# A two-layer graph kernel: scalar-tensor-tensor forms on VectorE, diagonal cells set among the incoming scatters, one branch on TensorE and GpSimd

## The chip, the core and the metric

The kernel runs on one core of one Trainium2 chip. The metric is the device time of one execution in microseconds, as the median of several runs. A core has TensorE (PE in the rows: matmul, with its weight loads as PEld), VectorE (DVE), ScalarE (ACT), GpSimd (POOL) and SyncE (SP), each with its own instruction stream, and 16 DMA engines. The streams meet only at semaphores. SBUF is the core's working memory, PSUM holds what TensorE accumulates, in 8 banks of 512 floats on each partition.

## What is computed

x has 1250 nodes of 1024 features, and there are 20,000 edges (src, dst), sorted by dst. Two layers follow each other, each with a residual and a layernorm.

```
def _sage_layer(h, edge_src, edge_dst, deg_inv, W_self, W_neigh, b):
    agg = jax.ops.segment_sum(h[edge_src], edge_dst, num_segments=h.shape[0])
    mean = agg * deg_inv[:, None]
    return h @ W_self + mean @ W_neigh + b
h = relu(_sage_layer(x, src, dst, deg_inv, W_self0, W_neigh0, b0))
x = _layernorm(x + _sage_layer(h, src, dst, deg_inv, W_self1, W_neigh1, b1))
# GCN layer over the same edges and one loop for each node
h = x @ W.T + b;  norm = deg_inv_sqrt[row] * deg_inv_sqrt[col]
x = _layernorm(x + segment_sum(norm[:, None] * h[col], row))
```

deg_inv is 1/max(number of incoming edges, 1), and deg_inv_sqrt comes from the out-degree plus one.

## The kernel before

The sums over edges are made dense. Two tables in HBM, `adj_in` and `adj_out`, hold for each pair of nodes how many edges there are; TensorE multiplies by them. A table has 1280 x 1280 cells, in five panels of 256 target nodes. All work is in float32 kept as a high and a low part (`hi`, `lo`: the rounded value, and what is left of it), so that one product takes three or two matmuls.

**GpSimd** builds the tables. It clears `adj_in` by four DMAs (`clear`), reads a flag that VectorE has computed (`general`: the edges are not of the usual kind; with these inputs it is 0), and then issues 160 indirect DMAs into `adj_in`, 125 cells each (`put`, line 643): ten groups g of 16. A group needs the indices that VectorE makes for it (`repeats(g)`, semaphore `batch_ready`). In the middle of group 0 it issues the four DMAs that clear `adj_out`. After group 9 it waits for `cleared_out`, sets the diagonal of `adj_out` to one by two DMAs of 640 single cells each (line 673), waits for both (`diagonal_set`), and issues 160 more scatters, into `adj_out`. "Incoming" and "outgoing" scatters are those into `adj_in` and `adj_out`. The scatters of groups 0 to 2, 3 to 6, 7 and 8, and 9 count on four semaphores, `scattered_in[0]` to `[3]` (`NEEDS`).

**TensorE** runs these stages in order: transposes of x with x @ W_neigh0 (`linear(N0, t)`, lines 1417 and 1446); x @ W_self0 turned (`self_turned`, 1472); the first mean by `adj_in` (`mean0`, lines 1492 and 1503) in four chunks of 2, 4, 2 and 2 tiles of 128 nodes, each with ten matmuls for the degrees and then eight blocks d of 128 features; the second layer's two weight products by seven products in place of eight, Strassen-like (`products(0)` and `products(1)`, 1560); the second mean (`mean1`, 1577); the GCN sum by `adj_out` (`gather`, 1594, in the same four chunks); and the GCN weights (`linear(GCN, t)`, 1417 and 1401). Mean0, mean1 and gather exist twice in the program, for the usual form and for the general one, which takes plain float32; TensorE branches on the flag at line 1641 ahead of mean0 and at line 1647 ahead of mean1 and gather. In both the general form stands first in the program, so the usual one is jumped to.

**VectorE** takes what TensorE accumulated and splits it: the low part is `tensor_tensor(value, hi, subtract)`. In mean0 it multiplies each block by 1/degree, which frees the PSUM bank (`h_free`), and adds the self part, which SP fetched (`s0_in`); TensorE may be six blocks ahead of it: `pe.wait_ge(h_free, m - 5)` for block m counted from 0, so its ninth block needs the third multiply. After the second block of chunk 0 VectorE also reduces a panel (line 1185). Ahead of the products and of mean1 TensorE waits for low parts (`right_lo`, `u1_lo_done`; lines 1074 and 1160).

**SP** loads in one fixed order. `load_chunk_1(c)` waits for the scatters that chunk c needs:

```
for b in range(c + 1):
    sp.wait_ge(scattered_in[b], 16 * RUN * (NEEDS[b] - (NEEDS[b - 1] if b else 0)))
load_panels(adj_in, c, m1_panels[c], m1_full)
```

Chunk 1 therefore needs groups 0 to 6, 112 scatters, and the fetches of the self part for mean0 stand behind it in SP's stream. The first load of `adj_out` waits for all 160 outgoing scatters (`scattered_out`) and for the ninth tile of mean1. ScalarE makes the high parts.

Of the kernel before, what the change touches and what calls it, by code (L numbers as in the profile page):

```python
# [6 lines left out]
T = 128  # L7
# [8 lines left out]
F32 = mybir.dt.float32  # L16
# [7 lines left out]
def build(nc, x, src, dst, w_self0, w_neigh0, b0, w_self1, w_neigh1, b1, w_gcn, b_gcn, out):  # L24
# [44 lines left out]
    with ExitStack() as ctx:  # L69
# [542 lines left out]
        def _(pool):  # L612
# [37 lines left out]
            with pool.If(general > 0):  # L650
# [12 lines left out]
            pool.wait_ge(cleared_in, 16 * 4)  # L663
            for g in range(GROUPS):
                pool.wait_ge(batch_ready, g + 1)
                for c in range(RUN):
                    put(adj_in, idx_in, mult, g * RUN + c, scattered_in[sum(g >= need for need in NEEDS)])
                    if (g, c) == (0, RUN // 2):
                        clear(adj_out, cleared_out)
# [5 lines left out]
            for j in range(EC):  # L675
                put(adj_out, idx_out, loops, j, scattered_out)
# [217 lines left out]
        def _(dve):  # L894
# [7 lines left out]

            def grouped(buf):
                return buf[0:EP, :].rearrange("p (g c) -> p g c", g=GROUPS)
# [6 lines left out]
            def split_lo(l, k):  # L911
                dve.wait_ge(w_hi_done, KD * l + k + 1)
                nc.vector.tensor_tensor(w_row(l, k, 1), raw_slots[raw_slot[l, k]], w_row(l, k, 0).bitcast(F32), ALU.subtract
                                        ).then_inc(w_lo_done, 1)
# [52 lines left out]
            def repeats(g):  # L967
# [5 lines left out]
                for k, (first, found) in enumerate(((0, before), (WINDOW + 1, behind))):  # L973
                    near = key[0:EP, g, first:first + RUN]
                    near = bass.AP(tensor=near.tensor, offset=near.offset, ap=[*near.ap, [1, WINDOW]])
                    nc.vector.tensor_tensor(eq, mine, near, ALU.is_equal).then_inc(same, 1)
# [95 lines left out]
            def right_low(n):  # L1072
                dve.wait_ge(right_hi, n + 1)
                nc.vector.tensor_tensor(right_op[n % 2][:, :, 1, :], rights[n // 7][n % 7], right_op[n % 2][:, :, 0, :].bitcast(F32),  # L1074
                                        ALU.subtract).then_inc(right_lo, 1)

            def left_sums(i):
# [4 lines left out]
                elif i == 1:  # L1082
                    dve.wait_ge(left_sum, 1)
                    nc.vector.tensor_tensor(a21, a11, a21, ALU.subtract).then_inc(left_sum, 1)
# [4 lines left out]
                else:  # L1089
                    dve.wait_ge(left_sum, 3)  # L1090
                    dve.wait_ge(left_lo, 2)
                    nc.vector.tensor_tensor(a12, a12, a11, ALU.subtract).then_inc(left_sum, 1)
# [586 lines left out]
```

## Time and profile before

| | us |
|---|---|
| median of 3 runs (lowest, highest) | 856.4 (853.21, 860.26) |
| the profiled execution, whole | 858.52 |
| its span, first to last instruction | 856.8 |
| TensorE busy | 833.5 (97%) |
| VectorE busy | 461.7 (54%) |
| GpSimd busy | 459.5 (54%) |
| ScalarE busy | 177.4 (21%) |

The mean granted clock of TensorE is 0.993 of its full 2.4 GHz. Times in the rows are us from the span's start. An engine's "idle before" is the time in which it did nothing ahead of an instruction, and behind the arrow stands what ended last before it started; where several semaphores are waited for, only the last one is named.

### The profile page before, as it was taken

The numbers are of one execution on the slowest core, as the hardware profiler recorded it, in microseconds if no ns is written. First come the engines' busy times: TensorE is split into PE (matmuls) and PEld (weight loads), VectorE is DVE, ScalarE is ACT, GpSimd is POOL, SyncE is SP. The second block draws the span as 40 slices with busy tenths as digits, with TensorE's granted clock in tenths as the row PEclk, the third lists the DMA queues.
The fourth block names the chain that finished last, engine by engine and source line by source line (L and its number), as shares of the span: only waits on it lengthen the run. The fifth ranks groups of instructions, "written<-read, shape, count | busy, mean of one in ns | idle before, by whom it ended". The sixth has DMA issues, their size and how long they took to land.

```text
span 856.8 us, 10998 instructions
## 1 busy us (share of the span) xinstructions
PE 833.5 (97%) x4295; PEld 710.8 (83%) x4295; DVE 461.7 (54%) x714; ACT 177.4 (21%) x218; POOL 459.5 (54%) x343
## 2 busy tenths in 40 slices
PE   8999999999999999999999999999979999999996
PEld 6888888888988899788888888778869889988885
DVE  6555659200017465897553678666663535455555
ACT  4111131111111113353223012222221122200000
POOL 5028886877778857888588688878830000000000
PEclk9999999999999999999999999999999999999998
DMA  9977965453786443768886579168757748655551
GB/s 334 379 294 277 341 197 154 136 161 89 196 256 166 111 86 102 258 238 282 291 292 217 219 262 292 33 192 228 214 183 263 224 144 282 210 197 197 196 191 44
DMA packets 99482, 180.56 MB, mean 211 GB/s; under 512 B 15474, under 2 KB 75898, under 8 KB 94048
## 3 DMA queue, kind: packets, MB, share of 16 engines
q1 hardware_dynamic: 60144, 124.17, 43.6%
q10 hardware_dynamic: 26896, 40.65, 13.4%
q0 software_dynamic: 12384, 14.95, 7.7%
q8 instruction: 38, 0.62, 0.3%
q14 instruction: 20, 0.16, 0.0%
HBM read 107.08 MB, written 72.43 MB: 210 GB/s over the span
## 4 chain that ended last, share of the span: by engine, by line
POOL 46%; PE 28%; issue 20%; DMA 3%; DVE 2%; POOLq 1%; ACT 0%; SPq 0%; DVEq 0%
POOL adj_out L643 25%; POOL adj_in L643 21%; PE ps L1417 13%; PE ps L1594 10%; PE ps L1446 2%; PE ps L1401 1%; DMA adj_out<-ones_nt 1%; POOLq L643 1%; DMA panel_tiles<-adj_out 1%; DMA raw<-in_L_gnn_W_neigh 1%; DVE sacc L1291 0%; PE ps L1358 0%; DMA adj_out<-loops,idx_out 0%; DVE wx L908 0%; PE ps L1616 0%
## 5 line engine op out<-in xcount | busy, mean ns | idle before, releaser
L643 POOL DMA_INDIRECT adj_out<-loops,idx_out x160 | 245.1, 1532 | 74.1 <-issue 65.8
L643 POOL DMA_INDIRECT adj_in<-mult,idx_in x160 | 198.7, 1242 | 89.2 <-issue 89.2
L1560 PE MATMUL ps<-u 128*128 128x512 f32 x840 | 190.7, 389 | 1.4 <-DVE u L1074 1.4
L1560 PEld LDWEIGHTS ps<-u 128*128 128x128 f32 x840 | 157.6, 188 | 34.3 <-issue 1.6
L1472 PE MATMUL ps<-wx 128*128 128x512 f32 (+1 forms) x576 | 109.7, 351 | 1.2 <-ACT outb L751 1.1
L1472 PEld LDWEIGHTS ps<-wx 128*128 128x128 f32 x576 | 94.0, 189 | 17.0 <-ACT outb L751 1.8
L1417 PE MATMUL ps<-u 128*128 128x512 f32 x432 | 98.2, 389 | 0.0
L1577 PE MATMUL ps<-u,panel_tiles 128*128 128x512 f32 (+1 forms) x400 | 93.9, 393 | 1.9 <-DVE s L1141 1.9
L1503 PE MATMUL ps<-wx,u 128*128 128x256 f32 (+5 forms) x640 | 95.3, 310 | 0.0
L1417 PEld LDWEIGHTS ps<-u 128*128 128x128 f32 x432 | 81.0, 188 | 16.8
L1503 PEld LDWEIGHTS ps<-wx,u 128*128 128x128 f32 (+1 forms) x640 | 87.4, 192 | 6.6
L1417 PE MATMUL ps<-wx 128*128 128x512 f32 x384 | 89.6, 392 | 0.0
L1577 PEld LDWEIGHTS ps<-u,panel_tiles 128*128 128x128 f32 (+1 forms) x400 | 74.5, 188 | 18.0 <-issue 2.3
L1417 PEld LDWEIGHTS ps<-wx 128*128 128x128 f32 x384 | 71.4, 188 | 14.6
L1594 PE MATMUL ps<-u,wx 128*128 128x512 f32 (+2 forms) x480 | 74.5, 317 | 0.0
L1594 PEld LDWEIGHTS ps<-u,wx 128*128 128x128 f32 x480 | 67.2, 191 | 6.6
L1171 DVE TENSOR_SCALAR dinv_row<-ps 128x256 f32<-128x256 f32 (+2 forms) x4 | 1.9, 479 | 88.3 <-PE ps L1492 88.3
L834 ACT ACTIVATE std<-mv,eps 128x1 f32<-128x1 f32 x20 | 5.9, 295 | 163.5 <-DVE mv L1015 163.5
L751 ACT ACTIVATE outb<-ps,b0c 128x512 f32<-128x512 f32 (+1 forms) x24 | 14.8, 617 | 95.7 <-PE ps L1472 87.8
L1335 DVE SCALAR_TENSOR_TENSOR outb<-ps,dscale,xin 128x1024 f32<-128x1024 f32 x9 | 11.6, 1285 | 40.2 <-PE ps L1417 40.2
L806 ACT ACTIVATE ht<-ht 128x256 f32<-128x256 f32 (+2 forms) x32 | 14.9, 466 | 84.1 <-DVE ht L1182 84.1
L993 DVE TENSOR_TENSOR u<-ps,u 128x1024 fp32r<-128x1024 f32 x10 | 12.2, 1224 | 35.0 <-ACT u L711 35.0
(170 smaller groups left out, 783.8 us busy)
## 6 DMA issues: line engine op xcount, KB each, us to landing
left_scr<-u SPq DMA_DIRECT2D x7, 2560.0 KB, 9.5
u<-left_scr SPq DMA_DIRECT2D x7, 2560.0 KB, 9.6
xt_scr<-wx ACTq DMA_DIRECT2D x10, 1024.0 KB, 9.9
u<-xt_scr SPq DMA_DIRECT2D x10, 1024.0 KB, 4.9
wx<-xt_scr SPq DMA_DIRECT2D x16, 512.0 KB, 3.7
adj_in<-u POOLq DMA_DIRECT2D x4, 1600.0 KB, 24.9
adj_out<-u POOLq DMA_DIRECT2D x4, 1600.0 KB, 15.4
wx<-adj_in SPq DMA_DIRECT2D x5, 1280.0 KB, 8.0
```

The lines of the kernel that those rows point to most:

```text
L643: pool.indirect_dma_start(table, bass.IndirectOffsetOnAxis(ap=index[0:EP, j:j + 1], axis=0), counts[0:EP, j:j + 1], None, bounds_check=CEL ...
L751: nc.scalar.activation(staged[i % 4][:, 0:width], ps[:, d, 0:width], ACT.Identity, bias=b0c[:, d:d + 1]).then_inc(s0_free, 1)
L806: nc.scalar.activation(cell, cell, ACT.Relu).then_inc(h_done, 1)
L993: nc.vector.tensor_tensor(u[:, :, t, 1, :], pair_bank(acc_pair(q, t)).rearrange("p (a j) -> p a j", a=2), u[:, :, t, 0, :].bitcast(F32), A ...
L1335: nc.vector.scalar_tensor_tensor(z, pair_bank(acc_pair(GCN, t))[:, :], dscale[:, t:t + 1], rest, ALU.mult, ALU.add).then_inc(acc_free, 1)
L1417: ins = nc.tensor.matmul(acc[:, cols], left_tile[:, t % 2, k, left * T:(left + 1) * T], w_row(q, k, right)[:, cols], start=(i == 0), stop= ...
L1446: ins = nc.tensor.matmul(pair_bank(acc_pair(N0, t))[:, cols], xs[:, t, k, left * T:(left + 1) * T], w_row(N0, k, right)[:, cols], start=(k ...
L1472: ins = nc.tensor.matmul(block_of[d], w[:, k, left, d * P:(d + 1) * P], where[right], start=(first and left + right == 0), stop=(final and ...
L1503: ins = nc.tensor.matmul(ps[:, h_bank(m), 0:width].rearrange("p (n j) -> p n j", n=n // 2), typed(u0_part(k, h, d), exact), typed(panels[0 ...
L1560: ins = nc.tensor.matmul(ps[:, product_bank(g, i, p), :], left_op[n % 2][:, p, k, left, :], right_op[n % 2][:, k, right, :], start=(not on ...
L1577: ins = nc.tensor.matmul(pair_bank(acc_pair("MEAN1", t))[:, cols], typed(p1_tile[t][0:rows(k), k, :], exact), typed(u[0:rows(k), n, k, h, ...
L1594: ins = nc.tensor.matmul(ps[:, g_bank(KD * c + d), 0:width].rearrange("p (n j) -> p n j", n=n // 2), typed(yd[:, h, d * P:(d + 1) * P], ex ...
```

## The change

Three things, and no other engine's stream is touched.

First, a helper `once(out, a, b, op)` issues `scalar_tensor_tensor(out, a, 1.0, b, mult, op)`, which is a * 1.0 op b, in place of `tensor_tensor(out, a, b, op)`. It is used in 124 instructions: the low parts of weights (24), of right operands (14) and of u1 (4), the comparison of keys (20), the additions of the self part (32), of bias and self rows (10 and 10), and the operand sums (10). Low parts read from PSUM, the left operands and the sums over the products stay as they were.

Second, GpSimd sets the diagonal ahead of group 5 of the incoming scatters. The wait for `diagonal_set` stays ahead of the outgoing scatters.

Third, TensorE branches once, ahead of mean0, and all later stages stand in both arms, the usual form first. GpSimd's branch likewise has the usual form of all its scatters in the first arm.

```diff
+            def scatter(general_form):
+                def diagonal():
+                    pool.wait_ge(cleared_out, 16 * 4)
+                    for i in range(2):
+                        cells = bass.AP(tensor=adj_out.tensor, offset=i * T * (PW + 1), ap=[[PW + 1, T], [PANEL + PW * PW, NT // 2]])
+                        pool.dma_start(cells, ones_nt[:, 0:NT // 2], allow_slow_non_contiguous=True).then_inc(diagonal_set, 16)
+
+                pool.wait_ge(cleared_in, 16 * 4)
+                for g in range(GROUPS):
+                    pool.wait_ge(batch_ready, g + 1)
+                    if g == GROUPS // 2:
+                        diagonal()
+                    for c in range(RUN):
+                        put(adj_in, idx_in, mult, g * RUN + c, scattered_in[sum(g >= need for need in NEEDS)])
+                        if (g, c) == (0, RUN // 2) and not general_form:
+                            clear(adj_out, cleared_out)
+                pool.wait_ge(diagonal_set, 32)
+                for j in range(EC):
+                    put(adj_out, idx_out, loops, j, scattered_out)
+
+            with pool.If(general == 0):
+                scatter(False)
+            with pool.Else():
+                clear(adj_out, cleared_out)
...
-            pool.wait_ge(cleared_out, 16 * 4)
-            for i in range(2):
-                diagonal = bass.AP(tensor=adj_out.tensor, offset=i * T * (PW + 1), ap=[[PW + 1, T], [PANEL + PW * PW, NT // 2]])
-                pool.dma_start(diagonal, ones_nt[:, 0:NT // 2], allow_slow_non_contiguous=True).then_inc(diagonal_set, 16)
-            pool.wait_ge(diagonal_set, 32)
...
+            def once(out, a, b, op):
+                return nc.vector.scalar_tensor_tensor(out, a, 1.0, b, ALU.mult, op)
...
-                nc.vector.tensor_tensor(cell, cell, fetch_slot(m)[:, 0:width], ALU.add).then_inc(h_sum, 1)
+                once(cell, cell, fetch_slot(m)[:, 0:width], ALU.add).then_inc(h_sum, 1)
...
-            with pe.If(general > 0):
-                mean0(True)
-            with pe.Else():
-                mean0(False)
-            products(0)
-            products(1)
-            with pe.If(general > 0):
-                mean1(True)
-                gather(True)
-            with pe.Else():
-                mean1(False)
-                gather(False)
-            for t in range(NT):
-                linear(GCN, t)
+            def later_stages(exact):
+                mean0(exact)
+                products(0)
+                products(1)
+                mean1(exact)
+                gather(exact)
+                for t in range(NT):
+                    linear(GCN, t)
+
+            with pe.If(general == 0):
+                later_stages(False)
             with pe.Else():
...
+                later_stages(True)
```

GpSimd's stream from its branch on, as a difference (branch, incoming scatters, clears, diagonal, outgoing scatters; the arm that the flag 0 takes):

```order
+L670 COMPARE_AND_BRANCH
 L643 DMA adj_in<-mult,idx_in 1638400x1 x9
 L636 DMA adj_out<-u 128x3200 x4
-L643 DMA adj_in<-mult,idx_in 1638400x1 x151
-L673 DMA adj_out<-ones_nt 128x5x1 x2
+L643 DMA adj_in<-mult,idx_in 1638400x1 x71
+L655 DMA adj_out<-ones_nt 128x5x1 x2
+L643 DMA adj_in<-mult,idx_in 1638400x1 x80
 L643 DMA adj_out<-loops,idx_out 1638400x1 x160
```

The two diagonal DMAs moved from behind the 160th incoming scatter to behind the 80th, so the 32 scatters of groups 5 and 6 that chunk 1 needs stand behind them.

TensorE's stream before, from the end of mean0's second arm to the start of the second mean (1560 are the products, 1577 and 1368 mean1 and the transposes in it):

```order
L1503 MATMUL ps<-wx,u 128x226 x100
L1643 UNCONDITIONAL_BRANCH
L1560 MATMUL ps<-u 128x512 x840
L1647 COMPARE_AND_BRANCH
L1577 MATMUL ps<-u,panel_tiles 128x512 x80
L1368 MATMUL ps<-ident,late 128x128 x8
```

The same place now, in the first arm (1515 is mean0, 1572 the products, 1589 and 1380 mean1):

```order
L1515 MATMUL ps<-wx,u 128x226 x100
L1572 MATMUL ps<-u 128x512 x840
L1589 MATMUL ps<-u,panel_tiles 128x512 x80
L1380 MATMUL ps<-ident,late 128x128 x8
L1589 MATMUL ps<-u,panel_tiles 128x512 x40
```

The second compare-and-branch is gone, and what follows it in the program is the form that runs. Line numbers of VectorE and TensorE are 10 to 13 higher in the changed kernel.

## Rows read from the trace of the kernel before

**Rows 1.** The page's part 1: busy us, share of the span, instructions.
```profile
PE 833.5 (97%) x4295; PEld 710.8 (83%) x4295; DVE 461.7 (54%) x714; ACT 177.4 (21%) x218; POOL 459.5 (54%) x343
```

**Rows 2.** PE's waits: us in total, times, longest.
```profile
PE ps L1594 <- DMA panel_tiles<-adj_out: 4.5, 1, 4.5
PE ps L1492 <- ACT outb L751: 2.0, 1, 2.0
PE ps L1577 <- DVE s L1141: 1.9, 1, 1.9
```

**Rows 3.** Two lines of PE's sequencer: durations in ns, starts in us.
```profile
L1641 PEldq COMPARE_BRANCH  x1: 3933/3933/3933, 236.3 to 236.3; - x1
...
L1647 PEldq COMPARE_BRANCH  x1: 5952/5952/5952, 532.1 to 532.1; - x1
```

**Rows 4.** PE's timeline: start us, us, instruction, idle before and releaser.
```profile
345.67 1.63 PE L1560 MATMUL ps<-u 128*128 128x512 f32 x6 [1.43 <-DVE u L1074]
...
538.26 0.93 PE L1577 MATMUL ps<-u,panel_tiles 128*128 128x512 f32 x3 [1.90 <-DVE s L1141]
...
642.69 2.61 PE L1594 MATMUL ps<-panel_tiles,wx 128*128 128x256 f32 x13 [4.50 <-DMA panel_tiles<-adj_out]
```

**Rows 5.** SP's timeline, 224 to 262 us.
```profile
240.70 2.33 SPq L425 DMA_DIRECT2D wx<-adj_in  x2
```

**Rows 6.** SP's waits: us in total, times, longest.
```profile
SPq L460 <- DMA adj_in<-mult,idx_in: 22.7, 3, 12.2
```

**Rows 7.** VectorE's timeline, 242 to 266 us.
```profile
259.75 0.42 DVE L1182 TENSOR_TENSOR ht<-ht,xin 128x256 f32<-128x256 f32 x1 [5.54 <-DMA xin<-s0t_scr]
260.09 2.81 DVE L1185 TENSOR_REDUCE dpart<-wx 128x10 f32<-128x2560 f32 x1
...
263.14 0.42 DVE L1179 TENSOR_TENSOR ht<-ps,dinv_row 128x256 f32<-128x256 f32 x1
```

**Rows 8.** PE's timeline, 262 to 268 us.
```profile
265.39 2.90 PE L1503 MATMUL ps<-wx,u 128*128 128x512 f32 x12
```

**Rows 9.** GpSimd's groups by line: xcount, busy us, mean ns, idle before.
```profile
L643 POOL DMA_INDIRECT adj_out<-loops,idx_out x160 | 245.1, 1532 | 74.1 <-issue 65.8 <-DMA adj_out<-ones_nt 8.3
L643 POOL DMA_INDIRECT adj_in<-mult,idx_in x160 | 198.7, 1242 | 89.2 <-issue 89.2
...
L673 POOL DMA_DIRECT2D adj_out<-ones_nt x2 | 1.8, 926 | 0.0
```

**Rows 10.** GpSimd's timeline: two stalls, the diagonals' wait, two slow scatters.
```profile
201.48 1.19 POOL L643 DMA_INDIRECT adj_in<-mult,idx_in  x1 [2.77 <-issue]
...
322.71 1.47 POOL L643 DMA_INDIRECT adj_out<-loops,idx_out  x1 [8.34 <-DMA adj_out<-ones_nt]
...
340.99 3.29 POOL L643 DMA_INDIRECT adj_out<-loops,idx_out  x1 [0.30 <-issue]
...
415.62 1.19 POOL L643 DMA_INDIRECT adj_out<-loops,idx_out  x1 [8.95 <-issue]
...
595.24 1.70 POOL L643 DMA_INDIRECT adj_out<-loops,idx_out  x1 [0.30 <-issue]
```

**Rows 11.** VectorE's timeline ahead of the products and of the second mean.
```profile
343.13 2.28 DVE L1074 TENSOR_TENSOR u<-raw,u 128x2048 fp32r<-128x2048 f32 x1
...
533.81 2.82 DVE L1160 TENSOR_TENSOR u<-u,u 128x2560 fp32r<-128x2560 f32 x1
```

**Rows 12.** VectorE's groups by line: xcount, busy us, mean ns, idle before.
```profile
L1147 DVE TENSOR_TENSOR spare<-spare,bias 128x1024 f32<-128x1024 f32 x7 | 8.5, 1218 | 2.2 <-DMA spare<-in_x 2.2
...
L938 DVE SCALAR_TENSOR_TENSOR mult<-mult,u 125x160 f32<-125x160 f32 x2 | 0.7, 325 | 0.1
...
L923 DVE TENSOR_TENSOR mult<-mult,loops 125x160 f32<-125x160 f32 x1 | 0.3, 326 | 0.0
```

**Rows 13.** VectorE's timeline during two of the slow scatters.
```profile
340.39 2.82 DVE L1069 TENSOR_TENSOR u<-ht,u 128x2560 fp32r<-128x2560 f32 x1 [4.22 <-ACT u L775]
...
594.59 1.28 DVE L1276 SCALAR_TENSOR_TENSOR wx<-outb,dscale,wx 128x1024 fp32r<-128x1024 f32 x1 [1.59 <-ACT wx L843]
```

More of the change, by code:

```diff
@@ L662, in _ @@
                 pool.wait_ge(prescattered, 16 * EC)
[L663 to L669, printed above, removed]
-            pool.wait_ge(cleared_out, 16 * 4)
-            for i in range(2):
-                diagonal = bass.AP(tensor=adj_out.tensor, offset=i * T * (PW + 1), ap=[[PW + 1, T], [PANEL + PW * PW, NT // 2]])
-                pool.dma_start(diagonal, ones_nt[:, 0:NT // 2], allow_slow_non_contiguous=True).then_inc(diagonal_set, 16)
-            pool.wait_ge(diagonal_set, 32)
-            for j in range(EC):
-                put(adj_out, idx_out, loops, j, scattered_out)
+                scatter(True)
         @block.scalar
@@ L975, in repeats @@
                     near = bass.AP(tensor=near.tensor, offset=near.offset, ap=[*near.ap, [1, WINDOW]])
-                    nc.vector.tensor_tensor(eq, mine, near, ALU.is_equal).then_inc(same, 1)
+                    once(eq, mine, near, ALU.is_equal).then_inc(same, 1)
                     dve.wait_ge(same, g * STEPS + 2 * k + 1)
@@ L1083, in left_sums @@
                     dve.wait_ge(left_sum, 1)
-                    nc.vector.tensor_tensor(a21, a11, a21, ALU.subtract).then_inc(left_sum, 1)
+                    once(a21, a11, a21, ALU.subtract).then_inc(left_sum, 1)
                 elif i == 2:
@@ L1091, in left_sums @@
                     dve.wait_ge(left_lo, 2)
-                    nc.vector.tensor_tensor(a12, a12, a11, ALU.subtract).then_inc(left_sum, 1)
+                    once(a12, a12, a11, ALU.subtract).then_inc(left_sum, 1)
             def right_sums(g, i):
@@ L1098, in right_sums @@
                     dve.wait_ge(block_in[slots[2]], 16 * (g + 1))
-                    nc.vector.tensor_tensor(b12[g], b12[g], b11[g], ALU.subtract).then_inc(right_sum, 1)
+                    once(b12[g], b12[g], b11[g], ALU.subtract).then_inc(right_sum, 1)
                 elif i == 1:
@@ L1106, in right_sums @@
                         dve.wait_ge(left_lo, 7)
-                    nc.vector.tensor_tensor(t2[g], b22[g], b12[g], ALU.subtract).then_inc(right_sum, 1)
+                    once(t2[g], b22[g], b12[g], ALU.subtract).then_inc(right_sum, 1)
                 elif i == 2:
@@ L1110, in right_sums @@
                     dve.wait_ge(right_lo, 7 * g + 1)
-                    nc.vector.tensor_tensor(b11[g], t2[g], b11[g], ALU.subtract).then_inc(right_sum, 1)
+                    once(b11[g], t2[g], b11[g], ALU.subtract).then_inc(right_sum, 1)
                 else:
@@ L1114, in right_sums @@
                     dve.wait_ge(right_lo, 7 * g + 2)
-                    nc.vector.tensor_tensor(b21[g], t2[g], b21[g], ALU.subtract).then_inc(right_sum, 1)
+                    once(b21[g], t2[g], b21[g], ALU.subtract).then_inc(right_sum, 1)
             def after_product(g, i, p):
@@ L1146, in stage_bias @@
                     dve.wait_ge(bias_full, 16)
-                nc.vector.tensor_tensor(stage[t % 3], stage[t % 3], bias[:, :], ALU.add).then_inc(stage_sum, 1)
+                once(stage[t % 3], stage[t % 3], bias[:, :], ALU.add).then_inc(stage_sum, 1)
             def add_self(t):
@@ L1155, in add_self @@
                     dve.wait_ge(*summed(1, 4, t - HALF))
-                nc.vector.tensor_tensor(s1[:, t, :], s1[:, t, :], stage[t % 3], ALU.add).then_inc(self_added, 1)
+                once(s1[:, t, :], s1[:, t, :], stage[t % 3], ALU.add).then_inc(self_added, 1)
             def u1_low(half, t0):
                 dve.wait_ge(u1_hi_done, 2 * half + t0 // HALF + 1)
-                nc.vector.tensor_tensor(u[:, half, t0:t0 + HALF, 1, :], u1[:, t0:t0 + HALF, half * HD:(half + 1) * HD],
-                                        u[:, half, t0:t0 + HALF, 0, :].bitcast(F32), ALU.subtract).then_inc(u1_lo_done, 1)
+                once(u[:, half, t0:t0 + HALF, 1, :], u1[:, t0:t0 + HALF, half * HD:(half + 1) * HD],
+                     u[:, half, t0:t0 + HALF, 0, :].bitcast(F32), ALU.subtract).then_inc(u1_lo_done, 1)
             for m, (c, d) in enumerate(H_BLOCKS):
```

6 lines of the change are left out of this document (2 added, 4 removed).

## The prediction

> **What bounds the kernel now.** I read the page first: TensorE is busy for 97% of the span, VectorE for 54% [rows 1]. An engine that full is the bound wherever it doesn't wait, so the second view is the list of its waits: 4.5 us at the first gather block, 2.0 us at the first matmul of the first mean, 1.9 us at the first of the second mean [rows 2]. Any gain of this change must come out of these 8.4 us. The third view is the branch itself: ahead of the 2.0 and the 1.9 us stand the two compare-and-branch rows of PE's sequencer, 3.93 and 5.95 us long [rows 3]. The releaser that the waits name there (ACT, DVE) is only the one that came last. The longest wait has another owner: GpSimd's 320 scatters, one after the other, then the panel load, then PE at 642.69 [rows 2, 4]. So two arms meet at the gather: PE's own work, which gets there at 638.19 (642.69 - 4.50), and GpSimd's scatters, at 642.69. **The end moves as the later arm moves**, and so the sum is made.
>
> **The first branch.** With the usual form first, PE falls into mean0 and the 2.00 us go. The trace shows no PE branch that falls through, so it is bounded by 0 and by the old 2.00; I take 0, because these two jumps are the only places where PE stands still with its operands there.
> The Trainium skill (Runtime: NRT & Kernel Launch, Instruction fetch mechanics) says that code is read ahead in sequence only, and that a taken branch to a page outside the window has to fetch it first. It speaks for the 0; by the opposite reading 1.4 us of the sum below would be missing.
>
> But who is next? SP issues the panels of chunk 1 at 240.70 [rows 5], after waiting up to 12.2 us for scatters [rows 6]: those of groups 0 to 6, the first 112. The fetches for the first additions queue behind that load on SP; VectorE gets the second of them only at 259.75, then reduces a panel for 2.81 us, and only its third multiply, 263.14 + 0.42 = 263.56, frees the bank for PE's ninth block [rows 7]. PE starts that block at 265.39 [rows 8]. The slack is 1.83 us. PE wants to come 2.00 us earlier, and the 112th scatter comes later, because the two diagonal DMAs (2 x 0.926 = 1.85 us of issue [rows 9]) now stand ahead of group 5. So VectorE is ready at 265.41, and PE's 2.00 us turn into a wait of 2.0 us there: **the first branch is worth nothing**. (The panel loads of chunks 2 and 3 wait for scatters in the same way; I give them no price, since the ninth block has then slowed PE by as much.)
>
> **The diagonals.** Their old wait (8.34 us [rows 10]) becomes a gap of 0.30 as between any two scatters: -8.04 on GpSimd's arm; the 1.85 us of issue are moved, not removed. The clears that they wait for were issued in the first group, and GpSimd should find that done. What has no row is a diagonal with scatters right behind it. Lower bound 0: scatters are issued at 1.5 us each with other DMAs in flight. Upper bound 8.04: the old wait, whole, in the new place. GpSimd does stall now and then without a semaphore, 39 scatters apart, 2.77 us at 201.48 and 8.95 us at 415.62 being two of six [rows 10]. One of them will fall near the diagonals and may last as long as their writes. I take 1.0, near the lower end, because 2.77 is already in the old sum and the diagonals are spent within a few scatters. I also take one more such stall, 2.8 us, which the old wait at 314 hid (range: none to two). GpSimd's arm: 642.69 - 8.04 + 1.0 + 2.8 = 638.4.
>
> **Product start.** PE waits 1.43 us there for VectorE's low half of the first right operand [rows 4]. One of the two operations ahead of it changes form; 0 by the price below.
>
> **The second branch.** Products end at 538.26 - 1.90 = 536.36. VectorE's second L1160 ends at 533.81 + 2.82 = 536.63 [rows 11], and PE needs it. From such an end to the matmul it takes 0.26 us (345.67 - 343.13 - 2.28 at the product start [rows 4, 11]), so PE starts at 536.89 instead of 538.26: -1.37, not -1.90. PE's arm: 638.19 - 1.37 + 1.0 (the stall of the diagonals, seen through the ninth block) = 637.8.
>
> **The scalar-tensor-tensor forms.** 124 VectorE instructions change. Time of one: at 125x160 the two forms take 326 and 325 ns; at 128x1024 the old form takes 1218 ns [rows 12] and the present three-operand one, with a scalar read from SBUF, 1.28 us [rows 13]. So 0 to 62 ns each; I take 0, since the 160-wide row has the immediate scalar that the change uses. Even at 62 ns it is 7.7 us on an engine that is idle for 46%, and of that about five instructions (0.3 us) lie ahead of the second mean.
> The other effect could be larger. A scatter takes 1.19 us unless VectorE runs an operation with two SBUF inputs: at 340.99 it took 3.29 us, until 344.28, with L1069 running from 340.39 to 343.21 [rows 10, 13]. Over 1.19 the outgoing scatters lose 160 x (1.532 - 1.192) = 54 us and the incoming ones 8 us [rows 9]. Does the new form free them? The present one does not: at 595.24 a scatter took 1.70 us, until 596.94, with the scalar-tensor-tensor L1276 running from 594.59 to 595.87 [rows 10, 13]. Both end 1.07 us after VectorE's instruction. So 0 here.
> The Trainium skill (SBUF — State Buffer, SBUF: two separate sides) speaks against this part: a VectorE instruction with two SBUF inputs takes the port pair that GpSimd shares, and the rule makes no difference between forms. The row at 595.24 agrees; by the rule the third case below is out, and its chance goes to the forecast.
>
> **The sum.** The gather starts at 638.4 instead of 642.69: -4.3 us. What follows the gather hangs on PE alone. The profiled execution took 858.52 us (span 856.8 and 1.7 around it), so 854.2. It lies 2.1 above the median of the runs, 856.4; I move the median by the same -4.3: **852.1 us**. Bounds of the unknown costs: no stall added at all, PE's arm at 636.8, so -5.9; two added stalls, GpSimd's arm at 641.2, so -1.5. That is 850.5 to 854.9 for this case.
>
> **Rivals.**
> Scatters held up by the diagonals (slower). If GpSimd must sit out the whole 8.04 us in the new place, the 112th scatter is 9.9 us late, VectorE frees the bank at 273.4, and PE loses 8.0 us in mean0. PE's arm: 638.19 - 1.37 + 8.0 = 644.8; GpSimd's: 642.69 + 2.8 = 645.5. The gather starts 2.8 us late: 859.2. It decides from a hold of 5.9 us (638.19 - 1.37 + 5.9 = 642.7). For it: the old wait was that long. Against: then it was a semaphore, now nothing but the queue.
> The immediate form frees GpSimd. The only long row of the new form has its scalar in SBUF; without that read it might not hold GpSimd. Then the incoming scatters win up to some 6 of their 8 us ahead of the 112th, which pays the 1.85, PE keeps its 2.0 us in mean0, and the outgoing scatters end tens of us early. All three waits go, 2.0 + 1.4 + 4.5 = 7.9: 848.5. Against: the rows of both forms hold.
> The branch does not do what it says. If falling through stalls PE as the jump did, PE's arm is 638.19 + 1.0 = 639.2 and the time 852.9. The branch rows would still be microseconds long.
>
> **How the numbers follow.** The forecast has 0.62, the held scatters 0.15, the freed port 0.12, the unchanged branch 0.06; 0.05 is left for what I don't see. The range takes in the first case with its bounds, the freed port, and most of the held scatters: 848.5 to 858.5. One per cent is 8.6 us, about what a measurement of this kernel can tell from no change (the three runs span 7.0). All 7.9 us that I can find lie within it: faster by over 1% needs the freed port and luck, 0.08; slower by over 1% needs a hold longer than any seen, 0.05; the rest, 0.87, is within.
>
> **What would show it.** PE: the compare-and-branch short, no idle time at the first matmul of mean0, but about 2 us or more at the ninth mean block (released by VectorE); 0.3 to 0.6 us at the first matmul of the second mean; under 1 us at the gather. GpSimd: no wait for the diagonals, a stall close behind them, outgoing scatters beginning some 5 us ahead of 322.71. VectorE: the same durations, and scatters during operations with two SBUF inputs still ending 1.07 us behind them; a mean well under 1532 ns for the outgoing scatters would be the freed port. I am wrong if the ninth block does not wait, or if the fetches behind chunk 1's panels come sooner than the scatters allow.

## The result, and the profile after

The changed kernel takes **849.35 us** (median of 20 runs, 847.52 to 851.96); the kernel before, on the same chip, 854.09 (20 runs, 849.98 to 860.26). The ratio is 0.9927, 95% interval 0.9908 to 0.9946. So it gained 4.74 us by the medians and 0.7% by the ratio (an estimate from all runs, which need not equal the quotient of the medians, here 0.9945): more than no change, less than one per cent. One run of the kernel before in the first group of experiments, 866.02 us, fell in a slower state of the chip and is left out of that group's numbers. The forecast, 852.1 from 856.4, was 4.3 us. That the two sums nearly agree is chance, as the traces show: the profiled execution went from 858.52 to 849.59, 8.9 us, twice the forecast, and in part by terms that the forecast did not have.

First the page of the changed kernel, part 1 (busy us, share of the span, instructions), which answers to [rows 1].

```profile
PE 830.6 (98%) x4295; PEld 707.9 (83%) x4295; DVE 461.3 (54%) x714; ACT 177.4 (21%) x218; POOL 459.1 (54%) x343
```

The same matmuls took PE 2.9 us less (833.5 before). Idle time that goes does not show in this column; matmuls that run faster do. That is the first sign of a term that is not a wait.

PE's waits in the changed kernel (us in total, times, longest), to be held against [rows 2]:

```profile
PE ps L1589 <- DVE u L914: 1.9, 1, 1.9
...
PE ps L1572 <- DVE u L914: 1.4, 1, 1.4
...
PE ps L1515 <- DVE ht L1191: 1.2, 1, 1.2
```

The wait at the gather (4.5) and the one at mean0's first matmul (2.0) are gone. The wait at the second mean is as long as before, 1.9, but not the same wait (below): now VectorE's low half is its releaser, and a new one of 1.2 us stands in mean0, at its ninth block. L914 is the line of `once`, so all its instructions have that one number.

What the waits don't say stands in the column PEclk of the windows, the granted clock. Stretches of the kernel before (us; busy time of PE, PEld, DVE, ACT, POOL with instructions; PEclk; DMA share; GB/s): behind the 2.0 us at mean0 and the next stretch, then behind the 4.5 us at the gather, and from the gather to the end.

```profile
240.70:244.00 3.30, 3.30 (x17) 3.30 (x17) 1.13 (x2) 1.17 (x3) 2.69 (x3) 0.50 0.80 174
244.10:247.50 3.40, 3.40 (x31) 3.40 (x30) 1.48 (x3) 0.15 (x1) 2.79 (x3) 1.00 1.04 338
...
643.40:646.70 3.30, 3.30 (x18) 3.30 (x17) 1.28 (x1) 1.15 (x1) 0.00 (x0) 0.50 0.74 201
642.69:856.80 214.11, 206.13 (x1140) 180.16 (x1140) 103.84 (x218) 26.11 (x51) 0.00 (x0) 0.98 0.57 195
```

And the changed kernel, the same places:

```profile
237.40:243.00 5.60, 5.60 (x49) 5.60 (x48) 2.71 (x4) 2.59 (x6) 4.38 (x5) 1.00 0.63 165
635.30:643.30 8.00, 8.00 (x68) 7.96 (x67) 5.47 (x13) 1.45 (x2) 0.00 (x0) 1.00 0.82 260
635.34:847.90 212.56, 204.54 (x1141) 178.58 (x1139) 107.69 (x229) 26.43 (x52) 0.00 (x0) 0.99 0.57 195
```

In the kernel before, PE ran at half the clock (0.50, the 1.2 GHz level) for 3.3 us behind each of the two idle times: 17 and 18 matmuls, where 3.4 us at full clock hold 31. In the changed kernel both places run at 1.00. At the gather the price can be read off whole: from its first matmul to the end took 214.11 us before and 212.56 after, **1.55 us** for the same work, beside the 4.50 of idle time. At mean0 it is about as much: from its first matmul (240.42 and 237.41, below) until PE was ready for the ninth block (265.39, and 262.19 - 1.20 = 260.99) PE took 24.97 us before and 23.58 after, 1.4 us less. Together that is the 2.9 us of the column above.

The new branch, as a row of PE's sequencer (durations in ns, start in us), against [rows 3]:

```profile
L1662 PEldq COMPARE_BRANCH  x1: 88/88/88, 235.4 to 235.4; - x1
```

88 ns where 3933 stood. PE's timeline of the kernel before at mean0's first matmul (start us, us, instruction, idle before and releaser):

```profile
240.42 2.31 PE L1492 MATMUL ps<-wx,ones_r 128*128 128x256 f32 x10 [2.00 <-ACT outb L751]
```

In the changed kernel the same matmul has no idle time ahead of it, and behind it stands the wait at the ninth block, against [rows 8]:

```profile
237.41 1.37 PE L1504 MATMUL ps<-wx,ones_r 128*128 128x256 f32 x10
...
262.19 2.12 PE L1515 MATMUL ps<-wx,u 128*128 128x512 f32 x8 [1.20 <-DVE ht L1191]
```

VectorE ahead of that wait, against [rows 7]:

```profile
258.32 0.43 DVE L914 SCALAR_TENSOR_TENSOR ht<-ht,xin 128x256 f32<-128x256 f32 x1 [4.12 <-DMA xin<-s0t_scr]
258.66 2.81 DVE L1197 TENSOR_REDUCE dpart<-wx 128x10 f32<-128x2560 f32 x1
...
261.71 0.42 DVE L1191 TENSOR_TENSOR ht<-ps,dinv_row 128x256 f32<-128x256 f32 x1
```

The third multiply ends at 262.13 and PE starts at 262.19: the chain that the forecast named, 1.4 us sooner than before (263.14 became 261.71), where the forecast had it 1.85 later.

GpSimd's timeline at the diagonals and at the first outgoing scatters, against [rows 10]:

```profile
186.77 1.19 POOL L643 DMA_INDIRECT adj_in<-mult,idx_in  x1 [0.30 <-issue]
187.95 1.84 POOL L655 DMA_DIRECT2D adj_out<-ones_nt  x2
190.10 1.24 POOL L643 DMA_INDIRECT adj_in<-mult,idx_in  x1 [0.30 <-issue]
...
311.27 1.19 POOL L643 DMA_INDIRECT adj_out<-loops,idx_out  x1 [0.30 <-issue]
```

No hold and no stall at the diagonals. The outgoing scatters begin 11.4 us sooner (322.71 before), not 5, and the last of them ends at 621.60 instead of 633.55. SP issues the gather's first panels at 625.53 instead of 635.39, as its timelines of the changed kernel and of the kernel before show:

```profile
625.53 0.36 SPq L425 DMA_DIRECT2D panel_tiles<-adj_out  x1
```
```profile
635.39 0.36 SPq L425 DMA_DIRECT2D panel_tiles<-adj_out  x1
```

Before, that load waited for scatters. Now they are done 3.9 us ahead of it, and SP waits there for PE, whose ninth tile of the second mean is the load's other condition.

Last the start of the second mean. VectorE and PE in the changed kernel, against [rows 11] and the second row of [rows 4]:

```profile
518.75 1.23 DVE L914 SCALAR_TENSOR_TENSOR spare<-spare,bias 128x1024 f32<-128x1024 f32 x1 [3.76 <-DMA spare<-in_x]
...
532.27 2.82 DVE L914 SCALAR_TENSOR_TENSOR u<-u,u 128x2560 fp32r<-128x2560 f32 x1
```
```profile
535.24 2.06 PE L1589 MATMUL ps<-u,panel_tiles 128*128 128x512 f32 x8 [1.94 <-DVE u L914]
```

PE arrives 3.06 us sooner than before (533.30 against 536.36), VectorE's second low half starts only 1.54 sooner (533.81 before). The row at 518.75 says why: VectorE stood for 3.76 us for a tile of x, which the kernel before got at 520.29 after 2.24 us, as its timeline shows:

```profile
520.29 1.23 DVE L1147 TENSOR_TENSOR spare<-spare,bias 128x1024 f32<-128x1024 f32 x1 [2.24 <-DMA spare<-in_x]
```

So the wait of 1.9 us has another cause than before. There VectorE's low half ended at 536.63, the compare-and-branch at 538.05 (532.1 + 5.952), and PE started at 538.26, 1.63 us behind VectorE [rows 3, 4, 11]: the jump held PE. Now PE starts 0.15 us behind VectorE's end (532.27 + 2.82 = 535.09). Of the 3.02 us by which the second mean starts sooner, 1.48 are the jump's and 1.54 are VectorE's earlier low half. That the wait has the same length is chance.

In the two profiled executions the 8.9 us come from: 3.02 at the start of the second mean (538.26 to 535.24), 4.33 more up to the first gather matmul (642.69 to 635.34 is 7.35: the 4.50 us of idle time, less 0.17 in small waits), and 1.55 of clock behind it. 3.02 + 4.33 + 1.55 = 8.90, and 856.8 - 847.9 = 8.9. About 0.8 to 1.0 of the 3.02 is there already when PE comes to mean0 (it arrives at 238.41 before, and passes without a stop at 237.41 after; a wait of 1.24 us in the first 10 us, behind a load of weights, is absent in the second); 0.6 of it stands there 28 us after the start, ahead of the branch and the diagonals.

### The profile page after: what moved, and what is told of

Same layout as the page of the kernel before. It is cut to its first block, busy times and chain, and to the rows that moved or that the text cites. A ratio compares the mean times of both kernels' runs of the same rounds, so it can differ in the third digit from the quotient of the medians.

```text
span 847.9 us, 11000 instructions
## 1 busy us (share of the span) xinstructions
PE 830.6 (98%) x4295; PEld 707.9 (83%) x4295; DVE 461.3 (54%) x714; ACT 177.4 (21%) x218; POOL 459.1 (54%) x343
## 4 chain that ended last, share of the span: by engine, by line
PE 61%; POOL 15%; DMA 9%; issue 8%; DVE 5%; SPq 1%; ACT 1%; POOLq 0%; ACTq 0%; DVEq 0%
PE ps L1572 19%; POOL adj_in L643 14%; PE ps L1429 12%; PE ps L1606 10%; PE ps L1589 9%; PE ps L1515 8%; DMA adj_in<-u 4%; DMA first_rows<-in_L_gnn_W_neigh 1%; DMA spare<-in_x 1%; DMA xin<-s0t_scr 1%; PE ps L1413 1%; DVE u L914 1%; PE ps L1380 1%; SPq L514 1%; DVE sacc L1303 0%
## 5 line engine op out<-in xcount | busy, mean ns | idle before, releaser
L643 POOL DMA_INDIRECT adj_out<-loops,idx_out x160 | 245.2, 1533 | 65.4 <-issue 65.4
```

What stands on the lines that cost most here:

```text
L643: pool.indirect_dma_start(table, bass.IndirectOffsetOnAxis(ap=index[0:EP, j:j + 1], axis=0), counts[0:EP, j:j + 1], None, bounds_check=CEL ...
```

## The experiments

All times are medians in us. Runs with the same "before" ran on the same chip, beside that kernel.

| run | median | lowest to highest | runs | before beside it | ratio, 95% interval |
|---|---|---|---|---|---|
| branch_only | 853.31 | 849.47 to 860.33 | 12 | 856.71 | 0.9966, 0.9931 to 1.0001 |
| diag_only | 851.22 | 849.55 to 856.58 | 12 | 856.71 | 0.9950, 0.9923 to 0.9977 |
| branch_diag | 850.51 | 849.01 to 853.16 | 12 | 856.71 | 0.9941, 0.9913 to 0.9970 |
| split_mean | 847.90 | 846.82 to 853.55 | 8 | 856.71 | 0.9904, 0.9867 to 0.9940 |
| late_diag | 851.16 | 848.58 to 854.53 | 10 | 856.11 | 0.9931, 0.9901 to 0.9962 |
| idle | 858.05 | 855.84 to 861.48 | 12 | 856.11 | 1.0011, 0.9983 to 1.0040 |
| idle_filled | 856.97 | 855.77 to 859.34 | 12 | 856.11 | 1.0008, 0.9980 to 1.0037 |
| all_three | 849.53 | 846.76 to 851.90 | 9 | 856.11 | 0.9916, 0.9882 to 0.9950 |
| after_again | 849.81 | 848.28 to 851.19 | 12 | 854.27 | 0.9938, 0.9912 to 0.9964 |
| branch_diag_again | 849.74 | 848.62 to 852.24 | 12 | 854.27 | 0.9934, 0.9908 to 0.9960 |
| split_again | 847.86 | 846.67 to 849.99 | 7 | 854.27 | 0.9907, 0.9873 to 0.9940 |
| split_prod | 848.39 | 846.40 to 850.61 | 8 | 854.27 | 0.9919, 0.9888 to 0.9950 |

My theory after the result: the gain is the gather's wait plus the half clock behind it, both taken away by the diagonals; PE's branch adds its 2 us and its half clock, of which later waits for VectorE take most back. The rivals: the forecast's own account (idle time alone, the branch worth nothing), and the new forms of VectorE.

**branch_only and diag_only** each put one part of the change into the kernel before.

```diff
 branch_only
-            with pe.If(general > 0):
-                mean0(True)
...
+            with pe.If(general == 0):
+                later_stages(False)
+            with pe.Else():
+                later_stages(True)
 diag_only
             for g in range(GROUPS):
                 pool.wait_ge(batch_ready, g + 1)
+                if g == GROUPS // 2:
+                    pool.wait_ge(cleared_out, 16 * 4)
+                    for i in range(2):
...
-            pool.wait_ge(cleared_out, 16 * 4)
-            for i in range(2):
...
             pool.wait_ge(diagonal_set, 32)
```

> The kernel before with PE's single branch alone, usual form first. Clock theory: mean0 starts some 2 us sooner, and its first matmuls, which ran 3.41 us at a granted clock of 0.5 in the kernel before, run at 1.0, which gives 1.5 us more; so PE stands 3 to 3.5 us ahead at its ninth block, waits 1 to 2 us there for VectorE, and is 1.5 to 3 us ahead after it. The end is 0 to 3 us sooner, by how long GpSimd keeps the gather waiting (in the profiled execution the wait of 4.5 us grows to 6 to 7.5, and the half clock behind it stays). Rival, as forecast: the ninth block gives back all of it, PE is 0 to 0.3 us ahead after it, the end 0.

> The kernel before with the diagonals moved among the incoming scatters, nothing else. Clock theory: the idle time of the gather goes (4.5 us in the profile of before) and with it the 3.41 us at a granted clock of 0.5 behind it (1.5 us); the half clock at mean0's start stays. 6 us under the profiled execution of before, 852.5; against the median of before 2 to 4 us less. Rival, as forecast: 4.3 us of idle time alone, 854.2 for the profiled execution, with a new stall of GpSimd of about 3.8 us by its diagonals.

The branch alone gave 853.31 from 856.71, with an interval that reaches 1; the diagonals alone 851.22, clearly faster. The rivals fail in both. In branch_only the ninth block gives back 0.8 us and not all: PE starts the products at 343.54, 2.1 us sooner than before (345.67), of which 0.4 were there ahead of mean0. diag_only's profiled execution took 851.33, under both expected times, and GpSimd has no stall by its diagonals. The spread says more than the medians: branch_only, like the kernel before, reaches past 860, diag_only ends at 856.58. In branch_only's profiled execution (850.34) the gather did not wait at all: its last outgoing scatter ended at 621.58, 12 us sooner than in the kernel before, though the diagonals stand where they stood. GpSimd waited less for the very same diagonal transfers; its timeline, against the 8.34 of [rows 10]:

```profile
317.27 1.24 POOL L643 DMA_INDIRECT adj_out<-loops,idx_out  x1 [4.41 <-DMA adj_out<-ones_nt]
```

The old wait is 4.4 us in one execution and 8.3 in another. It makes 3.9 of the 12 us; another 5.3 come from shorter stalls ahead of the 40th and 79th outgoing scatters (5.39 and 2.44 us, against 8.95 [rows 10] and 4.18). So GpSimd's arm varies by more than the gather's wait, which stood in the one execution and not in the other. The forecast took the 4.50 us of one profiled execution as a property of the kernel.

PE's waits in diag_only's profile, where both old branches still stand, and the stretch behind the first of them:

```profile
PE ps L1578 <- DVE s L1142: 2.2, 1, 2.2
...
PE ps L1493 <- ACT outb L752: 1.4, 1, 1.4
```
```profile
240.40:243.80 3.40, 3.40 (x29) 3.40 (x30) 1.92 (x2) 1.55 (x4) 2.79 (x3) 1.00 0.70 158
```

The idle time at the old branch was 1.4 us here and the clock stayed at 1.00 behind it: the half clock of the kernel before at that place is no fixed price of the jump. The expectation that it would stay in diag_only was wrong.

**branch_diag** has both parts, with VectorE's forms and GpSimd's branch as before.

> PE's single branch and the moved diagonals together, VectorE's forms and GpSimd's branch as in the kernel before. If the forms and GpSimd's branch are worth nothing: as the changed kernel, 849.4 give or take 1.5. Rival, the immediate form is quicker or frees GpSimd: 1 to 3 us above it.

850.51, 0.7 us under diag_only on the same chip, which is not clear of the noise (the means differ by 1.3 us, 95% interval -0.3 to 2.8). The two profiled executions differ by 1.7 us and show where: PE starts the products at 344.07 in diag_only and at 342.84 in branch_diag, VectorE's low half for the second mean ends at 535.32 and 535.09, and the second mean starts at 536.94 and 535.24. So of the first branch's 1.2 us only 0.2 are left where VectorE is the limit, and the rest of the 1.7 is the second branch: with it PE starts 1.62 us behind VectorE's end, without it 0.15. Against the changed kernel on another chip (849.35) branch_diag seemed 1.2 us slower, and so it was run again beside it:

> The changed kernel once more, beside the three below on the same chip: 849 to 850, granted clock 0.994 to 0.999, with no wait at the gather.

> PE's single branch and the moved diagonals without VectorE's forms and GpSimd's branch. If the forms and GpSimd's branch are worth nothing: within 1 us of the run beside it of the changed kernel. Rival, by the earlier runs on different chips (850.5 against 849.35): 1.2 us above it.

849.74 against 849.81. **VectorE's 124 new forms and GpSimd's branch are worth nothing** that these runs can tell (95% interval of the difference: 1.2 us either way), and the 1.2 us were the chip or the noise. The groups of the changed kernel say the same by themselves (xcount, busy us, mean ns): the old forms took 1218 and 2819 ns.

```profile
L914 DVE SCALAR_TENSOR_TENSOR u<-u,u 128x2560 fp32r<-128x2560 f32 x4 | 11.2, 2817 | 0.0
...
L914 DVE SCALAR_TENSOR_TENSOR spare<-spare,bias 128x1024 f32<-128x1024 f32 x7 | 8.5, 1217 | 3.8 <-DMA spare<-in_x 3.8
```

Nor does the immediate scalar free GpSimd. A scatter of the changed kernel during the new form at 532.27 to 535.09, and the group of the outgoing scatters, against [rows 9, 10]:

```profile
533.72 2.43 POOL L643 DMA_INDIRECT adj_out<-loops,idx_out  x1 [0.30 <-issue]
```
```profile
L643 POOL DMA_INDIRECT adj_out<-loops,idx_out x160 | 245.2, 1533 | 65.4 <-issue 65.4
```

533.72 + 2.43 = 536.15, 1.06 us behind VectorE's end, as before; the mean is 1533 ns against 1532.

**idle and idle_filled** measure the clock by itself. In both, SP loads the gather's first panels only when PE has ended the second mean, so that PE must wait for a load; in idle_filled PE runs 28 matmuls more meanwhile (their results are overwritten).

```diff
 idle
-            sp.wait_ge(acc_full, acc_index("MEAN1", NT - 2) + 1)
+            sp.wait_ge(acc_full, acc_index("MEAN1", NT - 1) + 1)
             load_panels(adj_out, 0, m2_panels[0], m2_full)
 idle_filled, besides
+                    if c == 0:
+                        pe.wait_ge(acc_free, acc_index("MEAN1", 8) + 1)
+                        for _ in range(28):
+                            nc.tensor.matmul(ps[:, g_bank(0), :].rearrange("p (a j) -> p a j", j=P), ones_r[:, :],
+                                             ones_r[:, :].unsqueeze(1).broadcast_to([P, BANK // P, P]), start=True, stop=True)
                     pe.wait_ge(m2_full[c], 16 * n // 2)
```

> The changed kernel, but SP loads the gather's first panels only when PE has ended the whole second mean: PE then stands idle for a load, 6.3 to 7.3 us. Clock theory: 849.4 + 6.5 to 7.3 of idle and 1.5 to 3.4 us more, since the matmuls behind run 3.41 to 6.8 us at a granted clock of 0.5: 857.5 to 860. Rival (idle time is lost once): 855.9 to 856.7.

> The kernel of the run idle, with 28 further matmuls of 512 columns ahead of the wait (about 6 us at 213 ns, into a bank that the gather overwrites). PE arrives and starts the gather at the same times. Clock theory: the granted clock stays at 1.0 and the end is 1.5 to 3.4 us sooner than in the run idle, near 856. Rival: the same time as the run idle.

Of idle, PE's timeline at the gather and the windows behind it, to 5 us and to the end:

```profile
645.01 1.22 PE L1606 MATMUL ps<-panel_tiles,wx 128*128 128x256 f32 x4 [6.51 <-DMA panel_tiles<-adj_out]
```
```profile
645.01:650.00 4.99, 4.99 (x23) 4.99 (x24) 1.28 (x1) 0.31 (x1) 0.00 (x0) 0.51 0.99 359
645.01:859.80 214.79, 206.81 (x1140) 180.81 (x1140) 103.24 (x217) 25.27 (x51) 0.00 (x0) 0.98 0.56 193
```

The same of idle_filled:

```profile
642.61 1.58 PE L1611 MATMUL ps<-panel_tiles,wx 128*128 128x256 f32 x11 [0.36 <-DMA panel_tiles<-adj_out]
```
```profile
642.60:647.60 5.00, 4.99 (x41) 4.99 (x42) 1.28 (x1) 0.10 (x1) 0.00 (x0) 1.00 1.00 371
642.61:855.30 212.69, 204.68 (x1140) 178.67 (x1140) 103.18 (x217) 25.06 (x51) 0.00 (x0) 0.99 0.57 194
```

23 matmuls against 41 in 5 us; 214.79 against 212.69 to the end. **2.1 us in the profiles are the clock's, at the same wait for the same load.** The medians differ by 1.1 us, under the 1.5 to 3.4 that I gave it and by themselves not clear of the noise (95% interval of the means' difference -0.2 to 2.2); but the granted clock of whole executions differs as well, 0.994 or less in 11 of idle's 12 runs, 0.995 or more in 10 of the 12 of idle_filled. The rival, that idle time is lost once, fails: PE that had been busy through the wait took the gather at full clock.

**late_diag** moves the diagonals from group 5 to the last group, behind the 112th scatter.

```diff
-                    if g == GROUPS // 2:
+                    if g == GROUPS - 1:
                         diagonal()
```

> The changed kernel with the two diagonal transfers ahead of the last group of incoming scatters (9), not of group 5, so behind the 112th scatter. By the forecast's step (two issues of 0.926 us ahead of the 112th make it 1.85 us late) the 112th scatter ends at 236.0, not 237.81, and the ninth block's wait of 1.2 us goes. Rival: the diagonals take the place of a stall that GpSimd has anyway at its 87th scatter (2.6 to 2.8 us where no diagonal stands there, none where one does); then the stall is back at the 87th, the 112th ends at 238 to 239 and the ninth block waits 0.5 to 1.2 us as it does. Time 848 to 849.5 either way.

851.16, not below the changed kernel (849.35 and 849.81 on other chips). GpSimd's timeline shows the stall of 2.8 us that the kernel before had at 201.48 [rows 10], back again. By the traces it stands ahead of the 88th incoming scatter; the expectation counted it as the 87th:

```profile
203.53 1.19 POOL L643 DMA_INDIRECT adj_in<-mult,idx_in  x1 [2.40 <-issue]
```

The 112th scatter ended at 240.6 (237.8 in the changed kernel), and PE waited longer at its ninth block, not less:

```profile
PE ps L1515 <- DVE ht L1191: 2.8, 1, 2.8
```

That the 112th scatter was 2.8 us later here is not the place of the diagonals: an earlier stall, ahead of the 49th scatter, took 4.07 us in place of 2.35, and the first scatter began 0.7 us later. The rival's numbers for this run (238 to 239, and 0.5 to 1.2 us) were missed by that much too. In all_three, with the same late diagonals, the 112th ended at 239.0, 1.2 us later than in the changed kernel after a start 1.3 us later. In all profiles with the diagonals ahead of group 5 there is no stall of a microsecond at the 88th scatter; where they stand elsewhere (before, branch_only, late_diag, all_three) it takes 2.4 to 3.0 us. So the diagonals take the place of that stall, and the 1.85 us that the forecast charged to the 112th scatter were paid out of it.

**split_mean and split_again** let the second mean start when the first five tiles of VectorE's low half are there.

```diff
-                    if t < 2:
-                        pe.wait_ge(u1_lo_done, 2 * n + 2)
                     cols = slice(n * BANK, (n + 1) * BANK)
                     for k in range(NT):
+                        if t < 2 and k % HALF == 0:
+                            pe.wait_ge(u1_lo_done, 2 * n + 1 + k // HALF)
```

> The changed kernel, where the second mean waits for VectorE's low halves by five tiles each, not ten. If its 1.9 us of idle time are a true wait for the second low half (ended 0.15 us before the matmul), they go: 1.9 us under the changed kernel, 847.4, with the gather still not waiting (its panels landed 3.3 us before they were needed). Rival: the wait is the jump's or comes back later (second halves, panels, the gather), 849.4.

> The changed kernel with the second mean's wait by five tiles: 1.5 to 1.9 us under the run beside it of the changed kernel, if the earlier 847.9 was the wait that went; the same time, if it was the chip.

847.90, and beside the changed kernel 847.86 against 849.81: **1.95 us less** (95% interval of the means' difference 0.6 to 3.2), about the whole wait. PE's timeline of split_again has no idle time left there, and the gather none either:

```profile
533.95 4.24 PE L1589 MATMUL ps<-u,panel_tiles 128*128 128x512 f32 x18
```

So the wait that is left in the changed kernel, where no jump stands, is VectorE's. Split_mean's own profile (853.55, the highest of its eight) met a wait of 2.1 us for VectorE's sums in the gather and ran at half clock twice; the other seven lie between 846.8 and 848.4.

**all_three and split_prod** add the start of the products: the matmuls that need the low half of the right operand stand behind the others of the first block (all_three has the late diagonals as well).

```diff
...
+                        if n == p == 0:
+                            steps = [(k, left, 0) for k in range(KH) for left in range(2)] + [(k, 0, 1) for k in range(KH)]
+                        for j, (k, left, right) in enumerate(steps):
+                            if n == p == 0 and j == 2 * KH:
+                                pe.wait_ge(right_lo, 1)
...
```

> The changed kernel with the late diagonals, the second mean's wait by five tiles, and the first product's low-half matmuls of the right operand behind the others (its 1.43 us wait for VectorE's low half). If each idle time is a true wait for VectorE alone, 1.4 to 1.9 us each: 846 (849.4 - 1.9 - 1.4), 845 if the ninth block's wait goes too; the gather's panels then land about when PE needs them. Rival: the gain of the product's start is given back at the next waits (the second operand's low half, the second mean): 847.5.

> As split_again, and the first product's matmuls that read the low half of the right operand stand behind its others, with the diagonals left at group 5. If VectorE's low half of the second right operand is the next limit (in the run all_three PE waited 1.07 us for it, in place of 1.43), 0.4 us or nothing under split_again; if the gain holds, 1.4 us under it.

848.39 against split_again's 847.86: nothing gained. The 1.43 us at the products' start became another wait for VectorE, and the one in the gather was longer, as PE's list in split_prod shows:

```profile
PE ps L1632 <- DVE sacc L1303: 2.1, 1, 2.1
...
PE ps L1577 <- DVE u L914: 1.1, 1, 1.1
```

VectorE's next low half came 1.1 us late, and its sums in the gather 2.1 (0.7 in the changed kernel). The second is not shown to follow from the edit: split_mean, which lacks it, had the same 2.1, and split_again 0.7. all_three (849.53, on another chip) shows the same two waits, of 1.1 and 1.4 us. **The version that beats both kernels is split_again: 847.86**, 0.75% under the kernel before by the medians, with a ratio of 0.9907.

## Why the prediction came out as it did

**Where the end is made.** Two arms meet at the gather, as forecast. Which of them is the later one was wrong: the forecast had GpSimd's at 638.4 and PE's at 637.8, and so tied the end to GpSimd. In the changed kernel PE's is the later, at 635.34. GpSimd's scatters end at 621.60, and with the 9.14 us that lay between their end and the gather before (642.69 - 633.55) they alone would let it start at 630.7, an estimate from these rows.

**The sum.** "Any gain of this change must come out of these 8.4 us", then "The gather starts at 638.4 instead of 642.69: -4.3 us" and "I move the median by the same -4.3": this is the step that failed, in three ways. First, it prices idle time alone and puts the clock behind it at nothing. 2.9 of the 8.9 us came out of PE's busy time: 1.55 behind the gather's wait, by which the end moved more than the gather did, and 1.4 behind mean0's. Second, the gather itself started at 635.34, 7.35 us sooner and not 4.3, since GpSimd's two added stalls (1.0 and 2.8) did not come, the branches gave PE more than -1.37, and PE was 0.8 to 1.0 us ahead already at mean0. Third, the 4.50 us of idle time belonged to the profiled execution, which lay 4.4 us above the median of the runs beside the result (858.5 against 854.1), not to the median run; the profiled execution of the changed kernel lies 0.2 above its median. A gain of 8.9 in that execution and of 4.74 in the median are one fact, and the first two errors against the third made the forecast of 4.3 come out near: luck. The chance of 0.87 for a change within 1% rested on this sum and on the step that one per cent is "about what a measurement of this kernel can tell from no change". The measured ratio is within 1%, but with 20 runs of each kernel its interval is 0.2% wide to either side and excludes no change.

**The first branch.** The idle time went and the compare-and-branch took 88 ns, as forecast. The rule of the Trainium skill (Runtime: NRT & Kernel Launch, Instruction fetch mechanics), that code is read ahead in sequence and only a jump out of what was read must fetch, agrees with the row of 88 ns; what the long rows before spent their time on no trace shows. "Worth nothing" was too low. The ninth block did wait for VectorE's third multiply, by the chain that was named, but 1.2 us, not 2.0, and not for the reason given: the 112th scatter did not come later. What the sum lacked is the half clock behind the 2.00 us, 1.4 us in that execution. PE kept 3.0 us up to the products (345.67 to 342.64), of which 2.2 are the branch's (2.00 + 1.4 - 1.2) and the rest was there ahead of it. At the second mean, where VectorE is the limit, about half of the 3.0 was left (1.54).

**The diagonals.** The 8.04 and their direction: right. The +1.0 for a hold and the +2.8 for a further stall did not come: there was no hold, the stall at the 88th scatter even went (-2.8), and the outgoing scatters began 11.4 us sooner, where some 5 were forecast. The rival of held scatters, 859.2, is out.

**The product start.** 1.43 us, unchanged: right.

**The second branch.** -1.37 was forecast, by VectorE's low half as the limit. Both were right for the step itself: PE starts 0.15 us behind VectorE's end, not 1.63, which is -1.48, and split_again shows the limit by removing it. What the working missed is that it held VectorE where it stood and let PE come at its old time: PE came 3.06 us sooner and VectorE, held by a tile of x, 1.54 sooner. So the second mean starts 3.02 us sooner, and PE waits 1.9 us for VectorE where 0.3 to 0.6 were forecast.

**The new forms.** 0 in duration and 0 for GpSimd: right on both, by the rows at 533.72 and by after_again against branch_diag_again. The rival of the freed port is out, though its time, 848.5, lies near the measured one: a time alone does not tell a mechanism.

**The gather.** "Under 1 us" of idle time: right, there is none, though the forecast let it be GpSimd's.

## What to carry to other kernels

Price an idle time of TensorE together with the granted clock of the stretch behind it, which the windows show and the list of waits does not; here one cost 4.50 + 1.55 us, while others of about 2 us cost nothing behind them. Before the longest wait of one profiled execution goes into a sum for the median, ask whether it ends on something that varies (a DMA behind a busy queue), and look at the spread of the times: the kernel before, whose two arms meet late, ran from 850 to 862, the changed one, whose GpSimd arm ends well ahead, from 847.5 to 852. An engine that is let go earlier by 3 us meets waits that had slack before, so the next limits on the other engine (here VectorE's low half) are worth a few lines; splitting that wait gave 1.95 us. And a wait of unchanged length can have changed its cause: look at what ended last in each of the two traces.

## What the runs showed of the hardware

The granted clock fell to 0.50 behind some idle times of PE and not behind others of the same length. It fell behind 2.0 and 4.5 us (before), 6.5 (idle), 2.8 at the ninth block (late_diag); it stayed at 1.00 behind 1.9 us at the second mean (before and changed), 2.2 us there and 1.4 at mean0 (diag_only). At the second mean of idle, behind 1.8 us for the same low half, it did fall, to 0.50 from 537.6 to 540.7: the same place and about the same idle time, with the other outcome. In split_mean it was 0.50 for 3.3 us in the part ahead of mean0, behind waits of about half a microsecond each:

```profile
219.30:222.60 3.30, 3.30 (x18) 3.30 (x17) 0.00 (x0) 0.00 (x0) 2.69 (x3) 0.50 0.67 184
```

while the changed kernel, with waits of the same length there, kept 1.00 (idle, all_three and branch_diag_again fell there too). What decides it stays open; no run here was made to tell it.

GpSimd's stalls among its scatters are not a fixed toll: the one ahead of the 88th incoming scatter (2.4 to 3.0 us in four profiles) is absent in the ten profiles in which two plain DMAs are issued behind the 80th. Why, no run shows.
